# The last stage of a four-layer network's last two batches as four jobs of 128 tokens, with its turns in transpose mode and a new order of work

## What is computed

```
q = x @ W_q.T                       # 2 halves x 4 heads x 64
sim = einsum(q, keys)               # 2 x 4 heads x 64 keys
sx, sy = top 8 of each half of sim; all_scores = sx[:, None] + sy[None, :]
scores, pk = top 8 of the 64 sums   # 8 of the 512 experts (index ix * 64 + iy, clipped at 512)
w = silu((x . down_embed[indices]) * softmax(scores))
out = sum(w * up_embed[indices]) + silu(x @ W_up.T) @ W_down.T
```

## Time and profile before

| | us |
|---|---|
| median of three runs | 1815.65 (1812.27 to 1816.45) |
| span of the profiled execution | 1807.1 |
| TensorE, VectorE, ScalarE, GpSimd busy | 1480.0, 1436.8, 1338.4, 1210.7 |

### The profile page before, as it was taken

The page is one execution under the profiler, slowest core; times in us unless marked ns, Lnnn a source line. Parts: engine busy times, 40 slices in busy tenths (PEclk is TensorE's granted clock), DMA queues, the critical chain, the costliest instruction groups (busy, mean ns, idle before and its releaser), DMA issues.

```text
span 1807.1 us, 27511 instructions
## 1 busy us (share of the span) xinstructions
PE 1480.0 (82%) x9545; PEld 1061.4 (59%) x9545; DVE 1436.8 (80%) x2200; ACT 1338.4 (74%) x2742; POOL 1210.7 (67%) x999
## 2 busy tenths in 40 slices
PE   5677677667899996676879999689899977899975
PEld 2343333345677775444557777566677755677854
DVE  4679999999988899889998778887998998611154
ACT  4468657757998887786788878798998887744453
...
GB/s 198 1 71 72 117 39 82 117 71 107 128 135 95 173 117 58 71 71 39 117 119 127 147 121 93 59 137 72 162 106 136 158 47 92 47 83 74 99 1 6
DMA packets 84585, 170.10 MB, mean 94 GB/s; under 512 B 9440, under 2 KB 14944, under 8 KB 84064
## 3 DMA queue, kind: packets, MB, share of 16 engines
...
## 4 chain that ended last, share of the span: by engine, by line
PE 46%; DVE 21%; ACT 17%; POOL 8%; issue 5%; DMA 2%; SPq 0%; DVEq 0%; POOLq 0%; ACTq 0%
DVE m L1052 9%; ACT m L1027 5%; PE ps L1444 5%; PE ps L966 5%; PE ps L1456 5%; DVE dtuB L1044 4%; ACT L345 4%; PE ps L1081 3%; PE ps L1183 3%; PE ps L1315 3%; POOL o L1670 2%; POOL o L1665 2%; PE ps L713 2%; ACT o L670 2%; PE ps L700 2%
## 5 line engine op out<-in xcount | busy, mean ns | idle before, releaser
L1062 POOL TENSOR_TENSOR m<-m 128x1024 f32<-128x1024 f32 x256 | 768.9, 3008 | 84.8 <-DVE m L1052 84.4
L1052 DVE TENSOR_TENSOR_SCAN m<-m,dtuB 128x1024 f32<-128x1024 f32 x256 | 584.9, 2285 | 18.6 <-ACT m L1027 5.6
L1027 ACT ACTIVATE m<-m,Aneg 128x255 f32<-128x255 f32 x1024 | 427.6, 497 | 24.5 <-DMA m<-m 23.2
L1044 DVE TENSOR_TENSOR dtuB<-m 128x1024 f32<-128x1024 f32 x256 | 342.5, 1338 | 13.1 <-DMA m<-m 5.0
L345 ACT ACT_TABLE_LOAD x188 | 241.2, 1283 | 3.3
L362 POOL TENSOR_TENSOR o<-o,mhalf 128x2 f32<-128x2 f32 x64 | 19.7, 308 | 222.1 <-DVE o L356 222.1
L1081 PE MATMUL ps<-m,w_const 128*32 128x256 f32 x2048 | 148.7, 415 | 5.7 <-POOL m L1062 5.7
L1425 ACT ACTIVATE o<-ps,w_mo 128x256 f32<-128x256 f32 x256 | 106.2, 471 | 51.0 <-PE ps L1448 50.9
L1444 PE MATMUL ps<-o 128*128 128x256 f32 x512 | 138.2, 392 | 6.8 <-ACT o L1425 5.2
L966 PE MATMUL ps<-m,wc 128*128 128x256 f32 x512 | 136.2, 425 | 6.2 <-ACT m L383 6.2
L1456 PEld LDWEIGHTS ps<-o 128*128 128x128 f32 x1024 | 128.6, 191 | 16.3 <-issue 4.9
...
## 6 DMA issues: line engine op xcount, KB each, us to landing
m<-m SPq DMA_DIRECT2D x256, 256.0 KB, 4.9
...
o<-in_mox SPq DMA_DIRECT2D x128, 256.0 KB, 3.4
...
```

What stands on the lines that cost most here:

```text
L1027: op = e.activation(dA[at % NA][:, j, 1:CH], R[q][:, h * CH + 1:h * CH + CH], ACT.Exp, scale=Aneg[:, l, 4 * g + j:4 * g + j + 1])
L1044: e.tensor_tensor(dtuB[:, :, :], bc(R[q][:, (2 + h) * CH:(3 + h) * CH].unsqueeze(1), 4, CH), Br[k % 2], ALU.mult).then_inc(S.dve, n.tick(f ...
L1052: e.tensor_tensor_scan(flat(G[at % NG]), flat(dA[at % NA]), flat(dtuB[:, :, :]), 0.0, ALU.mult, ALU.add).then_inc(S.dve, n.tick(f"s{g}"))
L1062: e.tensor_tensor(G[at % NG], G[at % NG], Cr[k % 2], ALU.mult).then_inc(S.pool, n.tick(f"c{g}"))
```

## The change

1. The `L3Ffn` of batches 6 and 7 is taken out of `todo` for them (`POST[:-1]`); in its place come four jobs of a new stage `L3Half`, one for each 128 tokens: the first half of batches 6 and 7 on lines a and b, the second on two new lines c and d (`Ps`). Lines c and d use the memory of the scan (`mem`) and the banks `ps[0:2]`, which were the scan's output and the front's bank, and the scan's tile `dtuB`. `L3Half` waits for the front's last step (lines c, d) and for `L3Attn` of its batch (`ready`). It does what `L3Ffn` does for one half, and writes its half out by a transfer of its own.
2. The norm helpers take a number of blocks.
3. The turns, in `L3Ffn` for batches 0 to 5 and in `L3Half`, are issued with `is_transpose=True`.
4. `ORDER` is new for all five engines, throughout.

The diff, cut to its core (of `ORDER` the last text lines; `norm_dve`, `norm_pool` and `norm_act` all take `v.blocks`; the parts of `L3Half` that are left out are those of `L3Ffn` with one half):

```diff
@@ -207,46 +207,46 @@
     dve = act = pool = sp = pe
 ORDER = {
     "sp":
...
-        "a3s2as2fsa2fsa4sasasfs3f2s2b2s2b2ab2f3sbsbs4b3s2ba7f3s8a2f3as8a2b5af3as7b3sb3ab3f3s2bs4bs5f3s5a12b12a14b3a2b14a",
...
+        "b2sfs4b4s3fa2s2as2af2sa4s2a3saf3s6b2s2b2aba4f2b2s7b3fb2s2f2sasa2s2a2s3f2as2f2a2s6bfb2a2f2b2sasb2s5bsb2fb4fsfsb2s7"
+        "f3s7a12b12a12ba2b2ab2ab11cbad",
     "pe":
...
-        "b2a2b7a3b4ab4ab7ab7a2ba2ba3b5a2b2a5b4a2b3a3b5",
...
+        "s2babab7asafb7f2sbfsf2a2b5ab2safb7f2a3fba4s2bf2a2ba5bsbfb3sba8b2a3b2ab2a2ba5sb2a4sb2afba3b2a3ba3b2a3babababab3aba"
+        "ba4baba2b2aba2b2aba2b3ab3ab3ababa2baba4babab2abab2aba2babab2ab5ab8ab11ca2cba3cbab6c3a2d6b2c2a3cd2cb3cd3",
     "dve":
...
-        "b7",
...
+        "abfa2s3a5safa2fab4ab2a2s3a2b2s2bsasba2babs4b9sa2bs3b2a3fafb6a4b10a6cab4aba2babdcac2a3b6ab3c3a3c2d3c2d3bc2bd2abd4b"
+        "cd",
     "act":
...
-        "b3ab2aba2bab2ab2ab3a2b4abab2ab2ab2a2babababa2b4a3b2aba2babab3a3b2a2bab6",
...
+        "aba4b2s2a5bab3a3b2a3b2a3b2ababab4a2b2a2bab3ab2abab4ab2ab3ababa2b2a2b2ababab3ab2ab2ab2ab3abc2a2b2ac2babab6c2daba2"
+        "d2abd3c2abc2badcdb2cd4",
     "pool":
...
-        "a4ba5bafs2a10b3sab7s5b10as2ba2b3a4b4a10b9a2ba8b10",
...
+        "s4bs2fs2a2fa2s6fa9s2asfbsfba6ba3sabfs2as3b5fbsb2fbsbas4b4ab2fb4s2bfs2as3fs5fs3bs3fbfs5fs4fsbs3fs5fs5fasa2sfas2bs2"
+        "bsa4ba5bafs2a9babsbabsb6s4b8abs2b2a2b3a3cab4da4b4a5bc4b2cbc4abdcd3bd6",
...
@@ -330,7 +330,13 @@
             return slice(i * 128, i * 128 + 128)
 
 
-        before, after = [None] * NB, [None] * NB
+        Ps = [line(f"o{2 + i}") for i in range(2)]
+        for i, T in enumerate(Ps):
+            T.mem = mem[:, i * MO_:(i + 1) * MO_]
+        Ps[0].banks = ps[0:2]
+        Ps[1].banks = [flat(dtuB[:, 2 * i:2 * i + 2, :]) for i in range(2)]
+
+        before, after, ready = [None] * NB, [None] * NB, [None] * NB
 
 
 
@@ -344,31 +350,33 @@
                 held[0] = kind
                 e.preload_act_table_set(SETS[kind])
...
 
-        def norm_views(v, V):
-            v.st, v.mv, v.ve, v.rs, v.nb = V.get(2, 6), V.get(2, 2), V.get(2), V.get(2), V.get(2)
+        def norm_views(v, V, blocks=2):
...
-            for i in range(2):
+            for i in range(v.blocks):
...
+            b = v.blocks
+            e.wait_ge(T.dve, n.dve(f"{p}mv{b - 1}"))
+            e.tensor_tensor(v.ve, v.mv[:, :, 1], mhalf[:, 2:2 + b], ALU.add).then_inc(T.pool, n.tick(f"{p}ve"))
+            e.tensor_tensor(v.nb, v.mv[:, :, 0], mhalf[:, 4:4 + b], ALU.mult).then_inc(T.pool, n.tick(f"{p}ng"))
...
@@ -1765,7 +1773,7 @@
-                            op = e.matmul(a[:, cut(k)], v.Em[h % 2][:, cut(k)], ident, start=h == 0 and k == 0, stop=h == 3,
+                            op = e.matmul(a[:, cut(k)], v.Em[h % 2][:, cut(k)], ident, is_transpose=True, start=h == 0 and k == 0, stop=h == 3,
                                           skip_group_check=True)
...
+        class L3Half(Stage):
+            def __init__(self, T):
+                v, V = self, Views(T.mem, MO_)
+                v.T = T
+                v.xn, v.xT = V.get(1, 128), V.get(128)
+                v.qT, v.sim, v.hid = V.get(4, 128), V.get(512), V.get(4, 128)
+                v.Em = [V.get(512) for _ in range(2)]
+                v.md = V.get(512)
+                v.wT = v.hid
+                v.t8, v.t8e, v.fl = V.get(8, 8), V.get(8, 8), V.get(4, 8)
+                v.ixu = v.fl.bitcast(U32)
...
+            def dve(self, e, n, c, i):
+                v, T = self, self.T
+                a, o = T.banks
+                Xi = X[:, 2 * c + i, :]
+                if n.dve():
+                    e.wait_ge(T.dve, n.dve())
+                else:
+                    e.wait_ge(F.dve, F.done(after[NB - 1][1]))
+                from_, job = ready[c]
...
+                yield from norm_dve(e, n, T, v, X[:, 2 * c + i:2 * c + i + 1, :])
+                e.wait_ge(T.act, n.act("sm"))
+                for g in range(8):
+                    e.max(v.t8[:, g, :], v.s3[:, g, :]).then_inc(T.dve, n.tick(f"t{g}"))
+                yield
...
+                for h in range(4):
+                    if h:
+                        e.wait_ge(T.pool, n.pool(f"w{h - 1}"))
+                    e.wait_ge(T.pool, n.pool(f"E{h}"))
+                    if h == 0:
+                        e.wait_ge(T.pe, n.pe("D"))
+                    e.scalar_tensor_tensor(v.md, v.Em[h % 2], v.s8[:, h, 7:8], o[:, :], ALU.is_ge, ALU.mult).then_inc(
+                        T.dve, n.tick(f"w{h}"))
+                    yield
+                    if h == 0:
+                        e.tensor_copy(v.d5, o[:, 511:512]).then_inc(T.dve, n.tick("d5"))
...
+            def pool(self, e, n, c, i):
+                v, T = self, self.T
+                norm_pool(e, n, T, v)
+                yield
+                e.wait_ge(T.dve, n.dve("mk"))
+                e.tensor_tensor(v.e64, v.al, v.msk, ALU.mult).then_inc(T.pool, n.tick("e"))
+                yield
+                e.wait_ge(T.act, n.act("ss"))
+                for p in range(2):
+                    if p:
+                        e.wait_ge(T.dve, n.dve("ri"))
+                        e.tensor_tensor(v.e64, v.e64, bc(v.rinv.unsqueeze(2), 4, 64), ALU.mult).then_inc(T.pool, n.tick("r"))
+                        e.wait_ge(T.pool, n.pool("r"))
+                        e.wait_ge(T.dve, n.dve("fl"))
+                        p4 = v.e64.rearrange("p h (a b) -> p (h a) b", b=8)
+                        e.tensor_tensor(p4, p4, bc(flat(v.fl).unsqueeze(2), 32, 8), ALU.mult).then_inc(T.pool, n.tick("p"))
+                        yield
+                    for h in (2 * p, 2 * p + 1):
+                        if p:
+                            e.wait_ge(T.pe, n.pe(f"t{h - 2}"))
+                        Eh = v.Em[h % 2].rearrange("p (a b) -> p a b", a=8)
+                        e.tensor_tensor(Eh, bc(v.s3[:, h, 0:8].unsqueeze(2), 8, 64), bc(v.s3[:, 4 + h, :].unsqueeze(1), 8, 64),
+                                        ALU.mult).then_inc(T.pool, n.tick(f"E{h}"))
+                        yield
+                    for h in (2 * p, 2 * p + 1):
+                        e.wait_ge(T.dve, n.dve(f"w{h}"))
+                        e.tensor_tensor(v.Em[h % 2], v.Em[h % 2], v.md, ALU.mult).then_inc(T.pool, n.tick(f"w{h}"))
+                        yield
+
+            def act(self, e, n, c, i):
+                v, T = self, self.T
+                a, o = T.banks
+                norm_act(e, n, T, v, X[:, 2 * c + i:2 * c + i + 1, :], v.xn)
+                yield
+                e.wait_ge(T.pe, n.pe("xT"))
+                e.copy(v.xT, a[:, 0:128]).then_inc(T.act, n.tick("xT"))
+                yield
+                e.wait_ge(T.pe, n.pe("q"))
+                e.copy(v.qT, o[:, :].rearrange("p (a b) -> p a b", a=4)).then_inc(T.act, n.tick("q"))
+                yield
+                e.wait_ge(T.pe, n.pe("sm"))
+                e.copy(v.sim, a[:, :]).then_inc(T.act, n.tick("sm"))
+                yield
+                table(e, "silu")
+                e.wait_ge(T.pe, n.pe("up"))
+                e.activation(v.hid, a[:, :].rearrange("p (a b) -> p a b", a=4), ACT.Silu).then_inc(T.act, n.tick("up"))
+                yield
+                table(e, "exp")
+                e.wait_ge(T.dve, n.dve("te"))
+                e.activation(v.t8e, v.t8e, ACT.Exp).then_inc(T.act, n.tick("te"))
+                e.wait_ge(T.dve, n.dve("ss"))
+                e.activation(v.sim, v.sim, ACT.Exp).then_inc(T.act, n.tick("ss"))
...
+            def pe(self, e, n, c, i):
+                v, T = self, self.T
+                a, o = T.banks
...
+                e.matmul(o[:, :], v.xT, w("l3f", "de"), start=True, stop=True).then_inc(T.pe, n.tick("D"))
+                yield
...
+            def sp(self, e, n, c, i):
+                T = self.T
+                e.wait_ge(T.dve, n.dve("x"))
+                e.dma_start(xout[:, 2 * c + i:2 * c + i + 1, :], X[:, 2 * c + i:2 * c + i + 1, :]).then_inc(out_done, 16)
                 yield
@@ -1793,7 +2004,7 @@
                 c = int(word[1])
                 if word[0] == "a":
                     before[c] = (T, sum(x[0] is T for x in todo) + 1)
-                todo += [(T, s, c) for s in (PRE if word[0] == "a" else POST)]
+                todo += [(T, s, c) for s in (PRE if word[0] == "a" else POST if c < NB - 2 else POST[:-1])]
         for c in range(NB):
             after[c] = (F, next(k for k, (b, l) in enumerate(UNITS) if b == c and l == NL - 1) + 2)
         for k in range(NU + 2):
@@ -1802,8 +2013,14 @@
             S.add(Scan(), k)
         for T, s, c in todo:
             T.add(stages[T.name][s], c)
+        for c in (NB - 2, NB - 1):
+            T = next(T for T, s, d in todo if d == c and s is L3Attn)
+            ready[c] = (T, len(T.jobs) - 1)
+            T.add(L3Half(T), c, 0)
+            P = Ps[c % 2]
+            P.add(L3Half(P), c, 1)
         Line.listed = True
-        lines = {"u": U, "s": S, "f": F, "a": Os[0], "b": Os[1]}
```

(3 more changed lines are left out.)

168 lines of the change are left out of this document (131 added, 37 removed).

## The result

The changed kernel takes 1989.74 us (1980.38 to 1996.96) against 1814.6 of the kernel before beside it: ratio 1.0955 [1.0925, 1.0986], 175 us **slower**. Forecast were 1801.2 us in a range of 1793 to 1812.

What follows compares the result with a forecast made beforehand. The last stretch was taken as latency-bound, with GpSimd idle 16.5 us between its products. Gains of 10.5 us there and 4 upstream, 14.5 together, from the 1815.65 us median gave 1801.2 us, range 1793 to 1812.

Steps and rivals of the forecast that it cites:

- Part 3: New order of turns before the last stage: scan nearly unaffected; 4 us gained upstream with halved turns, 4 lost to 9 gained.
- Rival 4: VectorE before 1480 us: scan steps wait behind other lines' turns, 0.6 us in each of 32 units; 1820 us, chance 0.11.
- At worst 4 us lost: Upstream bound: exponentials of the last two scan groups come after other lines' gelus and silus, making the last group late.
- Part 1: Last stretch: four half jobs in place of two fill GpSimd's waits; 10.5 us gained, with last turns 1.0 us cheaper.
- The head: Start of the last stretch: the first GpSimd product comes 3.5 us later, at 1741.0 us.
- the gaps: GpSimd's idle time between its products in the last stretch: 3.5 us in all, where 16.5 us were idle before.
- The one before b's `e`: GpSimd's wait for line b's first product in the last stretch, set by VectorE's block and mask: 3.2 us.
- rival 2: Last stretch: ScalarE's in-order queue takes GpSimd's place as limit; tail gain 4 us, upstream 3; 1809 us, chance 0.14.
- Part 2: TensorE's turns in transpose mode: instructions halved from 512 to 256, gaining 5.5 us at most upstream, 1.0 at the end.
- rival 1: TensorE's turns are not halved, because accumulating into the bank keeps two passes; 1806 us, chance 0.04.
- rival 3: TensorE's clock falls under transpose-mode turns, to 0.70 from 1480 to 1600 us; 12 us lost, 1813 us, chance 0.07.
- Table loads: ScalarE's activation tables: 182 loads instead of 188, at 1.28 us each, worth at best 7.7 us upstream.

Runs made afterwards that it cites:

- e13: e5 with 106 exchanges in VectorE's order, a line's turn put one place before a scan turn; 1910.77 us, ratio 1.0521.
- e14: e5 with 99 exchanges in VectorE's order, a scan turn put one place before a line's turn; 1918.38 us, ratio 1.0563.
- e6: e1 with SyncE's order new up to the last stage, the four compute engines' orders old; 1931.11 us, ratio 1.0612.
- e2: The kernel before (its stages, plain turns) with the new order for every turn up to the last stage; 1986.0 us, ratio 1.0943.
- e1: The changed kernel with the old order for every turn up to the last stage, then the new; 1814.57 us, ratio 0.9994.
- e5: e1 with the turns as plain matmuls instead of transpose mode; 1810.81 us, ratio 0.9969.
- e11: e5 with four unused 128x512 matmuls added behind the `down` product of line a's last stage; 1808.91 us, ratio 0.9957.
- e3: The kernel before with one edit, the turns issued in transpose mode; 1819.78 us, ratio 1.0017.

## Why the prediction was wrong

**Part 3 is the step that failed.** Its sentence "each engine's n-th scan turn has the same number of other turns before it, within one or two" was taken as nearly no difference, and "4 us gained" upstream came out as 175 lost. A difference of one place isn't small: e13 and e14 move 106 and 99 of VectorE's 512 scan turns by one place and lose 100 and 108 us. The new order gives 95 of them another count on VectorE, and on all engines but SyncE it costs 119 us. The count wasn't right either: 22 scan turns differ by more than two on VectorE (by up to 8), 2 on GpSimd (up to 6), and on TensorE the largest is 22, not ten. Counted in pairs of turns that change places, the old and the new order differ by 319 on VectorE, 76 on GpSimd, 744 on TensorE, 709 on ScalarE and 612 on SyncE, though none of VectorE's turns moves by more than 11 of its 1190 places. Not every such pair has a price: 119 us over the 1848 pairs of the compute engines is 0.06 us for each.

Rival 4 had the mechanism (a scan step behind another line's waiting turn), its chance of 0.11 leaned on the same count, and its price of 0.6 us per unit was 3.7 for the compute orders alone and 5.5 in all. Three things were missing from it. SyncE, whose order was not weighed, costs 117 us by itself (e6). The cost has two directions (e14): a line's turn held back by the scan is as dear. And part of it is no wait in any list but VectorE and GpSimd meeting in another sequence: 38 of e13's 97 us, though only 13 of the kernel after (L1052 has 355.5 us for 342.5). "At worst 4 us lost" was no bound: it priced only the last scan group. TensorE's clock falls with each of the bad orders as well (0.859 by the median of e2, which has plain turns, and 0.879 and 0.869 in e13 and e14, against 0.892). Whether that is a cause or follows from the waits no run separates, so the split of the 175 us between waits and clock stays open.

**Part 1, the tail: right in kind, too large.** From the end of the experts' last add to the end of the span were 86.5 us before and 80.6 in e1: 5.9 us gained, 10.5 forecast. GpSimd's groups, added up as in the earlier trace rows, cost 45.4 us in e1 (45.0 forecast), from first `e` to last product 54.7 (48.5 forecast, 61.5 before), and 7.5 behind it (7.1). The head came 1.5 us later, not 3.5. The mis-sized term is the gaps: 3.5 us forecast, 10.0 measured. The one before b's `e` is 6.25 us for 3.2. The forecast had it from VectorE alone, 2.7 us for b's block and 1.9 from the dense add to the mask. Both lengths were right, but VectorE stood before each of the two, first for b's scores, then for `down`, in e5:

```profile
1750.65 1.11 DVE L1825 MAX8 o<-o 128x8 f32<-128x64 f32 x8 [1.19 <-ACT o L1915]
...
1755.24 0.29 DVE L1838 TENSOR_TENSOR X<-ps,X 128x128 f32<-128x128 f32 x1 [1.88 <-PE ps L1970]
```

b's path through TensorE and ScalarE was given nothing. Most of these 3.07 us is TensorE's clock, as e11 shows (gap 4.1 us): the change itself turned this moment into one in which TensorE stands idle and then runs slowly. The other three waits are 1.9, 1.0 and 0.9 us, where 0.3 us were forecast. In e5, where the turns are as before, the whole kernel gains 0.31%, 5.6 us: the tail's gain and no more, and nearer to the 4 us of rival 2 than to 10.5. (The 1.27 us of the earlier trace rows that the forecast calls the mask product is L1607, the outer product.)

**Part 2, the turns: half right.** 256 instructions, a group of four at 0.60 to 0.66 us where the granted clock is 1.00 and 1.06 to 1.12 where it is 0.50, and rival 1 is out. But the 5.5 us upstream and the 1.0 at the end did not come (e3), and the clock fell with the edit: rival 3's mechanism, if at a smaller size. The 6.5 us missing and some 3 lost make about 10 us, an estimate from e3's ratio, where rival 3 had 12. That the lower clock is what took them is argued; no run has the transposes at the old clock.

**Table loads.** The new order has 182, as counted, the old one in e1 188; the 7.7 us that six loads are worth at most vanished in the 175.
